# Softmax denominators of layers 0 and 3: GpSimd adds the probabilities of two key tiles, and TensorE sums each pair once

## The reference, cut to what matters

```python
scores = einsum('bhqd,bhkd->bhqk', q, k) * scale      # masked
attn = softmax(scores, axis=-1)
out = einsum('bhqk,bhkd->bhqd', attn, v)              # then @ W_o + bias + residual
...
h = concatenate([x, latents], axis=1)                 # layer 3: 512 + 512 keys
attn = einsum('bkhd,bnhd->bhkn', q, kmat) / DH
```

## Time and profile before

| what | value |
|---|---|
| median of 3 runs | 4199.37 us (4190.5 to 4213.79) |
| the profiled execution: its own time | 4186.91 us |
| its span, first to last instruction | 4185.3 us |
| mean granted TensorE clock | 0.964 |
| attention loop of layer 0, first batch | 105.57 to 168.97 us |
| attention loop of layer 3, first batch | 787.20 to 919.00 us |

### The profile page before, as it was taken

The page is one execution under the profiler, slowest core; times in us unless marked ns, Lnnn a source line. Parts: engine busy times, 40 slices in busy tenths (PEclk is TensorE's granted clock), DMA queues, the critical chain, the costliest instruction groups (busy, mean ns, idle before and its releaser), DMA issues. The chain is left out here.

```text
span 4185.3 us, 39566 instructions
## 1 busy us (share of the span) xinstructions
PE 3692.9 (88%) x14128; PEld 1776.0 (42%) x14128; DVE 1524.4 (36%) x2792; ACT 1180.7 (28%) x1404; POOL 293.1 (7%) x228
## 2 busy tenths in 40 slices
PE   5898988889799898898979989889897998989989
PEld 2445543434344454343434445434343444533434
DVE  2415533540341553354034055335403405443530
ACT  1312323331131232333113123233412312423330
POOL 3000010100000001010010000100001000011000
PEclk9999999999899999999989999999998999999999
DMA  6322143511632214351163221535116222153501
GB/s 125 72 86 42 26 76 59 87 29 50 122 68 91 42 21 78 59 85 29 50 127 67 85 42 21 91 52 78 29 53 132 65 83 39 21 107 49 84 11 61
DMA packets 151761, 271.10 MB, mean 65 GB/s; under 512 B 15520, under 2 KB 22372, under 8 KB 151544
## 3 DMA queue, kind: packets, MB, share of 16 engines
q1 hardware_dynamic: 151556, 268.35, 31.6%
HBM read 152.95 MB, written 4.19 MB: 38 GB/s over the span
## 5 line engine op out<-in xcount | busy, mean ns | idle before, releaser
L922 ACT ACTIVATE pt<-score_banks 128x1024 f32<-128x1024 f32 x768 | 758.2, 1022 | 917.0 <-PE score_banks L783 480.2
L653 PE MATMUL bank<-xT,w 128*128 128x512 f32 x1664 | 750.4, 597 | 30.9 <-ACT xT L895 23.2
L1052 DVE TENSOR_REDUCE mcol<-bank 128x1 f32<-128x512 f32 x528 | 357.8, 688 | 361.1 <-PE bank L751 357.1
L653 PEld LDWEIGHTS bank<-xT,w 128*128 128x128 f32 x1664 | 313.2, 191 | 381.6 <-issue 361.1
L779 PE MATMUL score_banks<-qs,ks 99*128 99x512 f32 (+1 forms) x1280 | 434.3, 416 | 40.1 <-DMA qs<-nm_lo 22.7
L852 PE MATMUL score_banks<-w,wide 128*128 128x512 f32 x1024 | 443.4, 592 | 0.0
L1035 DVE TENSOR_REDUCE mcol<-score_banks 128x2 f32<-128x1024 f32 x248 | 302.0, 1223 | 321.6 <-PE score_banks L742 304.7
L751 PE MATMUL bank<-ks,qs 97*128 97x512 f32 (+1 forms) x784 | 337.0, 443 | 53.7 <-DVE mcol L1052 31.1
L1049 DVE CUSTOM_DVE_ANT_0 bank<-bank,wide 128x512 f32<-128x512 f32 x416 | 284.5, 707 | 257.7 <-PE bank L751 257.1
L779 PEld LDWEIGHTS score_banks<-qs,ks 99*128 99x128 f32 (+1 forms) x1280 | 236.1, 192 | 185.5 <-ACT pt L922 72.4
L1112 DVE TENSOR_TENSOR score_banks<-score_banks,r_down 128x512 f32<-128x512 f32 x32 | 22.4, 699 | 795.6 <-PE score_banks L852 795.6
(11 more groups left out here) (110 smaller groups left out, 2994.0 us busy)
## 6 DMA issues: line engine op xcount, KB each, us to landing
ks<-k_high SPq DMA_DIRECT2D x136, 256.0 KB, 5.7
w<-in_up SPq DMA_DIRECT2D x32, 1024.0 KB, 5.1
w<-in_down SPq DMA_DIRECT2D x32, 1024.0 KB, 5.3
qs<-q_high SPq DMA_DIRECT2D x112, 256.0 KB, 6.7
ks<-k_full SPq DMA_DIRECT2D x72, 256.0 KB, 7.1
w<-in_v SPq DMA_DIRECT2D x16, 1024.0 KB, 5.3
w<-in_q SPq DMA_DIRECT2D x16, 1024.0 KB, 7.9
qs<-q_full SPq DMA_DIRECT2D x64, 256.0 KB, 6.5
```

Of the source, the lines that this page charges most:

```text
L653: last = nc.tensor.matmul(o[:, :], wt[:, c, cols[0]:cols[1]], src[:, c, :], start=(c == 0), stop=(c == NC - 1))
L922: nc.scalar.activation(pt[:, i % PTB], score_banks[:, 2 * (i % 2):2 * (i % 2) + 2, :], ACT.Exp, scale=L.scale).then_inc(exp_done, 1)
L1052: ins = nc.vector.tensor_reduce(col, bank[:, :], AX.X, ALU.max)
```

## The change

In layers 0 and 3 (`PAIRED`) the probabilities get six places instead of four, two of them in `wide`. The product with v stays one step per key tile (`num`). GpSimd adds the probabilities of an even and the following odd key tile into one tile `pair_sum`, with two additions of 128x1024, one per score step. TensorE multiplies ones with that sum (`den`), half as many times as before. `den` of key tiles 2p and 2p + 1 stands behind `num` of key tile 2p + 2. The last one of a unit stands in the next unit's first group, ahead of its `num`, with `heads` behind it. Only ScalarE's copy of `num` keeps its place (`num_out`). The block `pair_sum` is single, so the first addition of a pair waits until the `den` before it has ended.

```diff
+PAIRED = (0, 3)
...
+        if n in PAIRED:
+            if kt == 0 and u:
+                steps += [("den", n, u - 1, L.kt // 2 - 1), ("heads", n, u - 1)]
+            steps.append(("num", n, u, kt))
+            if kt % 2 == 0 and kt:
+                steps.append(("den", n, u, kt // 2 - 1))
+            if kt == L.kt - 1:
+                steps.append(("num_out", n, u))
+        else:
+            steps += ([("pv_half", n, u, kt)] if n != 1 else []) + [("pv", n, u, kt)]
+            if kt == L.kt - 1:
+                steps.append(("heads", n, u))
+    if n in PAIRED:
+        steps += [("den", n, L.units - 1, L.kt // 2 - 1), ("heads", n, L.units - 1)]
...
+        pt_wide = wide[:, 0].rearrange("p (a b) s -> p a b s", a=2)
+        pair_sum = wide[:, 1]
...
+        def place(i):
+            _, n, u, s = SCORE_STEPS[i]
+            return (u * LAYERS[n].slots + s) % (PTB + 2 if n in PAIRED else PTB)
...
+        def wait_pt_free(eng, i):
+            _, n, u, s = SCORE_STEPS[i]
+            back = i - (PTB + 2 if n in PAIRED else PTB)
+            if back >= 0 and SCORE_STEPS[back][1] == n:
+                _, _, u, s = SCORE_STEPS[back]
+                if n in PAIRED:
+                    eng.wait_ge(num_done, N_NUM["num", n, u, s // 2])
+                    eng.wait_ge(pair_summed, 2 * N_DEN["den", n, u, s // 4] - 1 + s % 2)
...
+                        elif step[0] == "num" and step[3] % 2:
+                            _, n, u, kt = step
+                            d = N_DEN["den", n, u, kt // 2]
+                            first = SINDEX["score", n, u, 2 * (kt - 1)]
+                            if d > 1:
+                                pool.wait_ge(pv_done, N_PV[[s for s in STEPS if s[0] == "den"][d - 2]])
+                            for half in range(2):
+                                wait_probs(pool, first + 2 + half)
+                                nc.gpsimd.tensor_tensor(pair_sum[:, 2 * half:2 * half + 2, :], pt_of(first + half),
+                                                        pt_of(first + 2 + half), ALU.add).then_inc(pair_summed, 1)
...
+                        elif kind == "den":
+                            u, pair = step[2:]
+                            g = unit_at(n, u)
+                            if pair == 0 and g:
+                                pe.wait_ge(sums_out, g)
+                            pe.wait_ge(pair_summed, 2 * N_DEN[step])
+                            for j in range(4):
+                                last = nc.tensor.matmul(den[32 * j:32 * j + 32, :], ones[:, :], pair_sum[:, j, :],
+                                                        start=pair == 0, stop=pair == L.kt // 2 - 1)
+                            last.then_inc(pv_done, 1)
```

More of the change, by code:

```diff
@@ L161, in layer_steps @@
         steps += part[0:1] + ahead[0:1] + part[1:2] + ahead[1:2] + part[2:]
-        steps += ([("pv_half", n, u, kt)] if n != 1 else []) + [("pv", n, u, kt)]
-        if kt == L.kt - 1:
-            steps.append(("heads", n, u))
+        if n in PAIRED:
[12 more added lines that the diff above has]
+        steps += [("den", n, L.units - 1, L.kt // 2 - 1), ("heads", n, L.units - 1)]
     steps += [("o", n, t) for t in range(NT)]
@@ L322, in build @@
         exp_done, pv_done = sem("exp_done"), sem("pv_done")
+        num_done, pair_summed = sem("num_done"), sem("pair_summed")
         down_done = sem("down_done")
@@ L327, in build @@
         N_QK = order(("q", "k"))
-        N_PV = order(("pv",))
+        N_PV = order(("pv", "den"))
+        N_NUM = order(("num",))
+        N_DEN = order(("den",))
         N_MLP = {s: NT * i for s, i in order(("mlp_out",)).items()}
@@ L334, in build, with pt_of @@
                 N_DOWN[s] = downs
-        PV_OF = []
-        for _, n, u, s in SCORE_STEPS:
-            PV_OF.append(N_PV[("pv", n, u, s // 2)])
+        def place(i):
+            _, n, u, s = SCORE_STEPS[i]
+            return (u * LAYERS[n].slots + s) % (PTB + 2 if n in PAIRED else PTB)
+        def pt_of(i):
+            return pt[:, place(i)] if place(i) < PTB else pt_wide[:, place(i) - PTB]
+        def wait_pt_free(eng, i):
[6 more added lines that the diff above has]
+                    eng.wait_ge(pair_summed, 2 * N_DEN["den", n, u, s // 4] - 1 + s % 2)
+                else:
+                    eng.wait_ge(pv_done, N_PV["pv", n, u, s // 2])
+            elif n:
+                eng.wait_ge(pv_done, last_pv(unit_at(n - 1, LAYERS[n - 1].units - 1)))
         def wait_probs(eng, i):
@@ L367, in last_pv @@
             n, u = UNITS[g]
-            return N_PV[("pv", n, u, LAYERS[n].kt - 1)]
+            return N_PV[("den", n, u, LAYERS[n].kt // 2 - 1) if n in PAIRED else ("pv", n, u, LAYERS[n].kt - 1)]
         def at_count(g):
@@ L800, in _ @@
                                                         vone[:, kt, u // 2, u % 2 * 32:u % 2 * 32 + 32],
-                                                        pt[:, (i + j // 2) % PTB, j % 2, :],
+                                                        pt_of(i + j // 2)[:, j % 2, :],
                                                         start=kt == 0, stop=kt == L.kt - 1)
+                            last.then_inc(pv_done, 1)
+                        elif kind == "num":
+                            u, kt = step[2:]
+                            g, i = unit_at(n, u), SINDEX[("score", n, u, 2 * kt)]
+                            if kt == 0:
+                                wait_moved(pe, ("v", n, L.kt - 1))
+                                if g:
+                                    pe.wait_ge(values_out, values_count(g - 1))
+                            wait_probs(pe, i)
+                            wait_probs(pe, i + 1)
+                            for j in range(4):
+                                f0 = u * P + 32 * j
+                                last = nc.tensor.matmul(num[32 * j:32 * j + 32, :], v_at(n, kt)[:, f0:f0 + 32],
+                                                        pt_of(i + j // 2)[:, j % 2, :], start=kt == 0, stop=kt == L.kt - 1)
+                            last.then_inc(num_done, 1)
+                        elif kind == "den":
[4 more added lines that the diff above has]
+                            pe.wait_ge(pair_summed, 2 * N_DEN[step])
+                            for j in range(4):
+                                last = nc.tensor.matmul(den[32 * j:32 * j + 32, :], ones[:, :], pair_sum[:, j, :],
+                                                        start=pair == 0, stop=pair == L.kt // 2 - 1)
                             last.then_inc(pv_done, 1)
@@ L816, in _ @@
                             for j in range(4):
-                                rows, p_ = slice(32 * j, 32 * j + 32), pt[:, (i + j // 2) % PTB, j % 2, :]
+                                rows, p_ = slice(32 * j, 32 * j + 32), pt_of(i + j // 2)[:, j % 2, :]
                                 if kind == "pv_half":
@@ L919, in _ @@
                             act.wait_ge(score_full, i + 1)
-                            if i >= PTB:
-                                act.wait_ge(pv_done, PV_OF[i - PTB])
-                            nc.scalar.activation(pt[:, i % PTB], score_banks[:, 2 * (i % 2):2 * (i % 2) + 2, :],
+                            wait_pt_free(act, i)
+                            nc.scalar.activation(pt_of(i), score_banks[:, 2 * (i % 2):2 * (i % 2) + 2, :],
                                                  ACT.Exp, scale=L.scale).then_inc(exp_done, 1)
@@ L930, in _ @@
                                                      ).then_inc(values1_out, 1)
-                        elif kind == "heads":
+                        elif kind == "num_out" or (kind == "heads" and n not in PAIRED):
                             g = unit_at(n, step[2])
-                            act.wait_ge(pv_done, last_pv(g))
+                            if n in PAIRED:
+                                act.wait_ge(num_done, N_NUM["num", n, step[2], L.kt - 1])
+                            else:
+                                act.wait_ge(pv_done, last_pv(g))
                             nc.scalar.activation(at[:, step[2], :], num[:, :], ACT.Copy).then_inc(values_out, 1)
```

## The result

| | before | after |
|---|---|---|
| median | 4199.37 us (5 runs, 4186.95 to 4213.79) | 4236.89 us (5 runs, 4231.02 to 4243.79) |
| span of the profiled execution | 4185.3 us | 4235.2 us |
| mean granted clock | 0.964 | 0.950 |

The ratio after to before is 1.0093, with a 95% interval from 1.007 to 1.0117: the kernel is 0.9% slower. The forecast was 1.7% slower, 4269 us. Later runs of the kernel before have a median of 4196 us, so its profiled execution at 4186.91 was a quick one. That is why the two spans differ by 50 us and the medians by 37.5.

What follows compares the result with a forecast made beforehand. The prediction took TensorE, busy for 88% of the span, as the bound. Waits of 35.2 us against 24.3 gained per batch made 44 us, clock falls 26: 4199 + 70 = 4269 us, 1.7% slower, range 4200 to 4305.

Steps and rivals of the forecast that it cites:

- What the removed blocks give: TensorE in layers 0 and 3: 24 blocks fewer per batch and shorter waits at `heads` gain 24.3 us per batch.
- The chain of block and additions: From one `den` start to the next, at least the block, two GpSimd additions of 2.44 us and hand-overs must pass.
- C: Least time between `den` block starts: 6.1 us, or 9.3 with GpSimd's `heads` ahead of the additions.
- The wait at g8 of layer 3: TensorE's `den` behind `k(3)`: reached 2.8 us after the projection, sum ready after 7.8, wait 5.0 us.
- The sum of the waits: TensorE's new waits for GpSimd's sums: 13.4 us in layer 0, 21.8 in layer 3, 35.2 per batch.
- g10 of layer 0: `den` after a longer and a shorter group: TensorE has 7.3 us of work, wait 2.0 us.
- The clock: TensorE's clock falls behind six waits per batch of 3.3 to 5.0 us, costing 6.6 us per batch, 26 in all.
- The 0.9 at g8: Layer 3, behind `k(3)`: the clock fall costs 0.9 us, the next wait absorbing all but the `den` block.
- The 1.75: Layer 3's g12, behind `k(3, 1)`: the clock fall costs its full 1.75 us, as no new wait follows.
- short additions: Rival: GpSimd's additions take 1.53 us, mostly fixed cost, giving about 4177 us, or 4158 without clock falls; chance 0.10.
- A clock that falls behind waits of 1.9 us too: Rival: TensorE's clock falls more often, adding 14 us; 4290 us with slightly longer additions; chance 0.10.
- The clock staying up: Rival: TensorE works between the waits, so its clock does not fall and the time is 4243 us; chance 0.14.

Runs made afterwards that it cites:

- e1: Changed kernel with GpSimd's additions left out and ones multiplied with a constant tile, so the denominators are constants: 4091.38 us, 0.9751 of the kernel before.
- e3: Changed kernel with matmuls that add zero to the denominators put into the six longest waits of each batch: 4194.05 us, 1.0001 of the kernel before.
- e7: Changed kernel with `heads` and layer 3's k subtractions behind the additions on GpSimd, and each layer's last pair not added: 4117.52 us, 0.981 of before.
- e8: On top of e7, VectorE instead of GpSimd adds the pairs of the groups without maxima: 4114.04 us, 0.9798 of the kernel before.
- e2: Changed kernel with additions of 128x512 instead of 128x1024, odd heads' blocks taking their neighbour's sum: 4127.84 us, 0.9847 of the kernel before.
- e5: Changed kernel with GpSimd's two k subtractions of layer 3 put behind the additions of their pair: 4202.01 us, 1.0014 of the kernel before.
- e6: Changed kernel with the last pair of layers 0 and 3 not added, TensorE taking both key tiles directly: 4200.07 us, 1.0008 of the kernel before.

## Why the prediction came out as it did

- *What the removed blocks give* (24.3 us per batch): right. e1 gains 94 us by its span, 105 by its median, where 97 was said. Within it, layer 3 gave 12.6 per batch and not 15.2, where the grown DMA wait at g13 and the low clock behind it stand, and 2.8 came from layer 2. The changed kernel does not have that wait at g13.
- *The chain of block and additions*: right in place and nearly in size. C was put at 6.1 and 9.3 us, and the blocks are 5.92 and 9.1 apart. The wait at g8 of layer 3 was put at 5.0 and is 4.58, at g12 4.1 and 3.60, at the end 4.3 and 3.59 (layer 0: 3.33).
- *The sum of the waits*, 35.2 us per batch: mis-sized. The profile has 24.9 (99.4 over four), some 27 with 0.15 to 0.2 us at each of some ten blocks that does not show as idle (an estimate: a block is busy for 1.04 us, but the next matmul can start 0.89 after it). One part is the length of the chain: 0.2 us less at 14 places, 2.8 us. A second part is waits of layer 3 that show no idle time. At g10 (1.9) and g28 (1.0) TensorE came from a low clock and got to the block no earlier than the sum. At g18 and g24 (0.6 each) the blocks are the chain's 9.13 and 5.91 us apart, but TensorE had work until about then. A third is g10 of layer 0, put at 2.0 and measured 0.81: its group holds a `maxT` that waits 0.83 us for VectorE (at 147.99), and the prediction's group time left that out.
- *The clock*, 6.6 us per batch: right in kind and in all six places of all four batches, too small in sum. e3 shows 41 us, 10 per batch, of which 1.5 per batch are L1127. The 0.9 at g8 is right: 10.02 us to the next block against 9.13 in e3. At g26 it is 2.0 in three batches (0.9 in the fourth) in place of 0.9, since at the low clock TensorE's own work is longer than the chain (7.92 against 5.94). At g12 it is 5.4 in place of 1.75, of which 1.5 are not the clock. The 1.75 itself is a little more than the row behind it gives: a clock of 0.58 over 3.88 us loses 1.6.
- The two errors lie in the same places, and the clock partly replaced the waits. In layer 3 the waits are 15.0 us where 21.8 was said, and the low clock with L1127 costs 9.0 (by the blocks of e3) to 9.7 (by its whole stage) where 4.6 was said. That the total is right there, 10.8 against 11.2, is luck. Layer 0 was put 2.1 us too high, as its five waits were 9.5 us and not 13.4.
- *What was in no step*: 2.6 us per batch gained between the output projections of layers 1 and 2, whose code is unchanged. In e1, e3, e7 and e8 this stretch is as short, 152.1 to 152.5 us. In the first batch the two kernels run alike there for 59 us, to within 0.02 us. They part at a wait for `q_full`, 1.42 us before the change and 0.58 after. Behind it the kernel before has a stretch on the low clock,

```profile
615.00:619.00 4.00, 3.73 (x8) 2.05 (x8) 1.52 (x4) 0.00 (x0) 0.00 (x0) 0.57 0.95 137
```

and the kernel after has none at that point:

```profile
616.00:620.00 4.00, 3.41 (x12) 2.01 (x12) 2.75 (x5) 0.00 (x0) 0.00 (x0) 1.00 1.09 130
```

Three of the four batches before have this low stretch and take 155.5 us; the fourth has none there and takes 153.6. What moved it wasn't tried and stays open. These 10 us are part of the distance between 4269 and 4237. Layer 0's 2.1 us per batch make 8 more. The rest is mostly that the profile of before was some 10 us under its median, so a profile-to-profile difference of 50 shows as 37.5 to 40 in the medians.
- *The rivals*: short additions would have turned the sign, and e2 shows that they do; their length of 2.37 us decided against it. A clock that falls behind waits of 1.9 us too did not show: in the changed kernel's loops, from g2 on, no low stretch stands behind a wait under 2.7 us. The clock staying up would have left the kernel at the level of before (e3), not at 4243.

## What to carry to other kernels

When work moves from a full engine to an idle one, reckon the chain from the result's last reader to its next one, not the idle engine's load: GpSimd was busy for 18% of the span, and its chain still held TensorE up in some ten places of each batch. Look at what stands ahead of the moved work in that engine's own order; reordering two kinds of step and not moving the last piece of each layer turned 0.9% slower into 1.9% faster. And measure a change inside the stretch that it touches: the gain from e7 to e8 shows in the loops, but not beyond the noise of the medians. A wait of 2.7 us or more cost TensorE more than its length here, since the clock fell behind it, so breaking one long wait can be worth more than the idle time shows.

## What the runs showed of the hardware

A small VectorE instruction was held up by GpSimd's addition. L1127 is a maximum of two 128x16 SBUF tiles. Before the change it takes 0.175 us in all 8 executions, and after:

```profile
L1127 DVE TENSOR_TENSOR mcol<-mcol x8: 175/901/1627, 853.0 to 4052.2; 128x16 f32<-128x16 f32 x8
```

Four of the eight are long, one per batch, all at the place shown above. In the timeline there it starts at 853.00 and ends at 854.63, and the GpSimd additions that started at 849.93 end at 854.60. The other runs show that it waits for just the addition under way: it takes 0.34 us in e2, 0.20 in e3, e5 and e7, 0.55 in e8 and up to 2.06 in e6, and in each of them it ends 0.03 us after the GpSimd addition during which it started. In e3 this is the first addition of the pair, and the second is already under way.

The same happens the other way round. In e8, where GpSimd's multiplication starts at 157.17 during VectorE's first addition of a pair, it takes 2.11 us in place of 1.27, and VectorE's second addition takes 2.31 in place of about 1.2. The Trainium skill has this in "SBUF — State Buffer", section "Who interferes with whom": a VectorE instruction with two SBUF inputs contends with a GpSimd instruction that reads SBUF, for a shared pair of ports that is an exclusive lock. The traces agree, by the figures above. VectorE's maxima read out of PSUM while GpSimd adds keep their 0.69 us.

The reach of the clock was unexpected too: filling six waits per batch with 63 us of useless matmuls made the kernel 1% faster than leaving them idle.

And the length of one wait does not tell whether the clock falls. The prediction took 1.81 us as a length behind which it stays up. In the same trace, at the start of layer 0's loop, it falls behind 1.83 us, with 0.54 us of idle time shortly before. The granted clock is 0.52 from 110 to 113 us:

```profile
107.92 0.74 PE L779 MATMUL score_banks<-qs,ks 99*128 99x512 f32 x2 [1.83 <-ACT pt L922]
...
111.13 1.95 PE L822 MATMUL bank<-pt,ones 128*32 128x512 f32 x8
```

In e3's second batch it falls at g12 of layer 0, behind waits of 0.80 and 1.44 us that stand 5.92 us apart:

```profile
1198.28 1.33 PE L877 MATMUL bank<-wide,ones 128*32 128x512 f32 x8 [1.44 <-POOL wide L665]
```

```profile
1199.00:1202.00 3.00, 3.00 (x14) 0.89 (x7) 1.69 (x3) 0.36 (x1) 0.45 (x1) 0.50 0.03 5
```

In the changed kernel it stays at 1.00 behind the same two waits. What makes the difference these runs do not show.
